# The third batch's mix as seven products, and where its sums and its normalisation stand

## The chip, the cores and the metric

One core of a Trainium2 chip runs the whole kernel in one launch. The metric is device time in microseconds (us). TensorE is written PE, VectorE DVE, ScalarE ACT, GpSimd POOL and SyncE SP, as in the profile.

## The reference

Four batches of 512 rows and 512 columns go through a gated attention block and a gated feed-forward block:

```
q = ctx Wq^T + bq;  k = ctx Wk^T + bk          (256 -> 128)
att = softmax(q k^T)                           (512 x 512)
x = x + tanh(g0) * (LN(x) att^T-mixed over rows: einsum 'bln,bmn->blm')
w = ternary_quant(W): mean(|W|) * clip(round(W / mean(|W|)), -1, 1)
x = x + tanh(g1) * (silu(LN(x) wu^T) * (LN(x) wg^T)) wd^T     (512 -> 2048 -> 512)
```

## The kernel before, in words

Every engine has its program written out by hand, in the order in which it runs, and semaphores with constant counts order the engines against each other. An instruction that waits holds back all that stands behind it on its engine. SP issues all DMAs, transposes included, in one queue.

**Attention, batch by batch.** In batch `b` PE projects the context of batch `b + 1` (`project`, L724), transposes the last tile of the probabilities of `b` (`transpose_p`, L749), computes four tiles of energies of `b + 1` (`energy`, L738), and mixes the rows of `b`. ACT copies the transposed probabilities out of PSUM (`copy_at`, L1111), adds the biases of the next q and k (`bias_qk`, L1095), takes exponentials (`exp_row`, L1102) and scales them (`norm_p`, L1107). Between these ACT sums the absolute values of the weights for the ternary scale (`sum_abs`, L1088), rounds and signs them (L1118, L1124) and makes the high halves of the feed-forward's input (`high_t`, L1143). DVE takes row maxima (`row_max`, L1473), reciprocals of the row sums (`row_rsum`, L1477), mean and variance of the rows coming in (`rows_in`: L1484, L1490) and going out (`stats2`, `aggregate2`, L1515 and L1521; two tiles together in `rows_out`), adds the mix to the rows, normalises (`norm_x1`, L1529) and makes the low halves (`low_t`, L1547). POOL computes the factors of the normalisations in short dependent steps (`rstd1`, `rstd1_two`, `rstd2`, `rstd2_two`).

**The mix** of a batch is a product of 512x512x512 in float32. In the last two batches it is plain: `mix(b, i)` for four row tiles, each of 4 matmuls of 512 columns (L765), and DVE adds a tile of 512 columns (`make_x1`, L1495). In the first two (`b < NS`) it is done in quarters as seven products in place of eight (`mix_product`, L788: 4 matmuls of 256 columns each), in the order `MIX`; each product's result is added with factor `tanh * rstd` to the x tiles by two instructions of 256 columns (`add_mixed`, L1507; `s_xe` counts 14 in a batch). Products 5, 6, 7 and 3 have a sum of quarters of x^T on the left (`x_sums_1`, `x_sums_2`), 5, 6, 7 and 4 one of quarters of the probabilities on the right (`p_sums_1`, `p_sums_2`); POOL makes these eight sums of 512 columns. Products 1 and 2 need no sum.

**Bridge to the feed-forward.** Its input, the normalised x of all four batches, is also cut in quarters with seven products. The quarters and their sums (B11, B21, B22, T1 to T4) are cast to a high half by ACT (`high_t`) and a low half by DVE (`low_t`), and each is transposed by two DMAs (`transpose_block`, L466). POOL makes T3's and T1's differences (L639, L641; semaphores `s_t3`, `s_t1`), DVE those of T2 (L1647) and T4 (L1622). SP also loads W_down in four pieces (`load_down`), x^T tiles (`load_xt`) and writes x tiles of batches 2 and 3 back to DRAM (`spill`, L442). In `T_ORDER` the blocks are B11, B21, T3, T1, T2, B22, T4, and ACT's, DVE's and SP's programs follow it.

**Feed-forward.** From `product1(0)` on PE multiplies with ternary weights (L872, L874) and, from the fourth unit on, the hidden values with W_down. `product3(0)` is the first that waits for ACT's `copy_5(0)` (L1299), which stands behind `copy_1(0)`, T4's high half and a half of a sign on ACT; `copy_1(0)` in its turn waits for T4's difference.

The places on which the change bears, in PE's loop and in ACT's, which the change leaves as it is:

```
if i == 0: act.wait_ge(s_t3, 1); high_t(0, "T3", t3_sb)        # b == 2
if b == 2 and i == 1: act.wait_ge(s_t1, 1); high_t(0, "T1", xf_half(1, 0))
if i == 1: sum_abs(2, 2)                                       # then copy_at, exp_row(3, 3)
if b == NS and i < 2: pe.wait_ge(s_xe, 14 * NS)                # mix(b, i)
```

## Time and profile before

| | us |
|---|---|
| three runs: median (lowest to highest) | 396.78 (396.38 to 397.04) |
| the profiled execution, its own time | 397.08 |
| its span | 395.3 |
| PE busy | 389.9 |
| DVE busy | 314.4 |
| ACT busy | 266.7 |
| POOL busy | 169.3 |
| DMA, mean | 111 GB/s |

The attention of the four batches stands in the first 94 us, the feed-forward behind it. The granted TensorE clock is full in all slices. A busy share is a mean over stretches with different limits; what a step costs is read from the timeline of the engines around it. All times inside the kernel are given from the start of the span.

### The profile page before, as it was taken

Reading aid. Unit: us, or ns where it says so; the run is one execution under the profiler, and the core shown is the slowest. Engines: PE = TensorE matmul, PEld = TensorE weight load, DVE = VectorE, ACT = ScalarE, POOL = GpSimd, SP = SyncE. Lnnn points to the kernel's source line nnn. Section 1 sums busy time; section 2 is a strip of 40 time slices with the busy share of each in tenths; the row PEclk is TensorE's granted clock in tenths of the full one; section 3 lists DMA queues with packets and bytes.
Section 4 is the critical chain, followed back from the end, with each engine's and each line's share of the span. In section 5 each row is a group of like instructions: output and inputs, shape, how many; then the busy total and the mean of one; then the engine's idle time right before and its main releaser. Section 6 shows DMA issues by size and latency. Waiting matters only on the chain.

```text
span 395.3 us, 6059 instructions
## 1 busy us (share of the span) xinstructions
PE 389.9 (99%) x1944; PEld 214.9 (54%) x1952; DVE 314.4 (80%) x475; ACT 266.7 (67%) x360; POOL 169.3 (43%) x187
## 2 busy tenths in 40 slices
PE   8999999999999999999999999999999999999997
PEld 6566775454444444444444444444445565656886
DVE  0768897888899985879897875786869989798974
ACT  3786989889778786869788863746377566654400
POOL 0686826657875013222347002435359446271000
PEclk9999999999999999999999999999999999999999
DMA  7999967598500030030009643041500000000014
GB/s 286 409 413 414 389 210 174 151 266 211 162 2 0 1 108 0 2 107 0 2 0 225 117 79 61 1 167 73 165 22 1 2 2 2 0 2 0 2 55 159
DMA packets 43183, 43.91 MB, mean 111 GB/s; under 512 B 30992, under 2 KB 33168, under 8 KB 41104
## 3 DMA queue, kind: packets, MB, share of 16 engines
q1 hardware_dynamic: 43152, 43.53, 35.4%
q8 instruction: 16, 0.26, 0.3%
q14 instruction: 15, 0.12, 0.1%
HBM read 29.89 MB, written 6.29 MB: 92 GB/s over the span
## 4 chain that ended last, share of the span: by engine, by line
PE 75%; DVE 7%; issue 6%; ACT 5%; POOL 3%; DMA 2%; SPq 1%; DVEq 0%; POOLq 0%; ACTq 0%
PE pair L872 22%; PE pair L874 22%; PE pair L946 14%; PE pair L990 11%; PE pair L788 3%; DMA xf<-in_wdT 2%; PE pair L738 1%; ACT sh L1102 1%; DVE small L1473 1%; PE pair L724 1%; PE pair L803 1%; DMA xf<-in_first 1%; SPq L466 1%; DVE small L1515 1%; DVE xf L1674 1%
## 5 line engine op out<-in xcount | busy, mean ns | idle before, releaser
L872 PE MATMUL pair<-xb_hi,w_sb 128*128 128x512 f16 x448 | 169.8, 379 | 0.4 <-ACT xf L1299 0.2
L874 PE MATMUL pair<-xb_lo,w_sb 128*128 128x512 f16 x448 | 169.8, 379 | 0.0
L872 PEld LDWEIGHTS pair<-xb_hi,w_sb 128*128 128x128 bf16 x448 | 43.8, 98 | 52.9 <-ACT xf L1299 1.1
L874 PEld LDWEIGHTS pair<-xb_lo,w_sb 128*128 128x128 bf16 x448 | 43.8, 98 | 51.1 <-issue 0.3
L1250 ACT ACTIVATE xf<-xf,small 128x512 f32<-128x512 f32 x48 | 34.5, 720 | 52.3 <-DVE xf L1669 31.6
L946 PE MATMUL pair<-x_sb,sh 128*128 128x512 bf16 x248 | 55.1, 379 | 0.4
L1674 DVE SCALAR_TENSOR_TENSOR xf<-xf,small 128x512 f32<-128x512 f32 x48 | 40.0, 836 | 8.4 <-ACT xf L1250 8.4
L946 PEld LDWEIGHTS pair<-x_sb,sh 128*128 128x128 f16 x256 | 24.9, 98 | 30.6 <-DVE x_sb L1711 0.9
L604 POOL TENSOR_TENSOR w_sb<-w_sb 128x512 bf16<-128x512 bf16 x8 | 9.6, 1197 | 63.0 <-ACT w_sb L1124 63.0
L1679 DVE TENSOR_TENSOR sh<-xf,sh 128x512 f16<-128x512 f32 x36 | 32.1, 898 | 0.7 <-ACT sh L1261 0.7
L1725 DVE SCALAR_TENSOR_TENSOR x_sb<-pair,small,x_sb 128x256 f32<-128x256 f32 (+1 forms) x57 | 25.5, 472 | 5.9 <-PE pair L990 5.4
L1711 DVE SCALAR_TENSOR_TENSOR x_sb<-pair,small,x_sb 128x512 f32<-128x512 f32 x32 | 23.9, 747 | 7.8 <-PE pair L946 7.7
L1261 ACT ACTIVATE sh<-xf 128x512 f16<-128x512 f32 x36 | 22.1, 623 | 10.5 <-DVE xf L1674 9.3
L697 POOL TENSOR_TENSOR xf<-xf 128x512 f32<-128x512 f32 x7 | 9.9, 1409 | 44.2 <-DMA xb_lo<-xf 28.1
L765 PE MATMUL pair<-sh,xt_sb 128*128 128x512 f32 (+2 forms) x80 | 28.6, 508 | 0.0
L1664 DVE TENSOR_TENSOR xf<-pair,xf 128x1024 f32<-128x1024 f32 x16 | 19.5, 1221 | 8.8 <-PE pair L874 8.6
L1669 DVE TENSOR_TENSOR xf<-pair,xf 128x1024 f32<-128x1024 f32 x16 | 19.5, 1220 | 4.1 <-PE pair L874 3.9
L1659 DVE TENSOR_TENSOR xf<-pair,xf 128x1024 f32<-128x1024 f32 x16 | 19.5, 1220 | 4.1 <-issue 1.6
L1287 ACT ACTIVATE xf<-pair 128x1024 f32<-128x1024 f32 x16 | 16.4, 1023 | 8.1 <-PE pair L874 7.6
L765 PEld LDWEIGHTS pair<-sh,xt_sb 128*128 128x128 f32 x80 | 13.9, 190 | 12.6 <-issue 10.5
L1674 DVE SCALAR_TENSOR_TENSOR c<-c,small,pair 128x512 f32<-128x512 f32 x16 | 11.9, 742 | 10.1 <-ACT c L1250 10.1
L1118 ACT ACTIVATE w_sb<-w_sb,small 128x1024 f32<-128x1024 f32 x16 | 18.9, 1227 | 0.0
(198 smaller groups left out, 715.9 us busy)
## 6 DMA issues: line engine op xcount, KB each, us to landing
w_sb<-in_wugT SPq DMA_DIRECT2D x8, 1024.0 KB, 14.7
x_sb<-in_x SPq DMA_DIRECT2D x4, 1024.0 KB, 11.3
xf<-in_wdT SPq DMA_DIRECT2D x4, 1024.0 KB, 6.6
xt_sb<-in_wdT SPq DMA_DIRECT2D x4, 1024.0 KB, 5.0
xt_sb<-in_xT SPq DMA_DIRECT2D x12, 256.0 KB, 6.1
x_dram<-x_sb SPq DMA_DIRECT2D x8, 256.0 KB, 3.3
out<-x_sb SPq DMA_DIRECT2D x8, 256.0 KB, 2.0
x_sb<-x_dram SPq DMA_DIRECT2D x2, 1024.0 KB, 5.5
```

The lines of the kernel that those rows point to most:

```text
L765: last = pe.matmul(ps_x[i % 2][:, lo:hi], xt_tile(b, i)[:, k, :], at[:, k, lo:hi], start=(k == 0), stop=(k == KD - 1))
L872: pe.matmul(dst[:, m * 512:(m + 1) * 512], w[:, o:o + P], hi[:, k], start=start and k == 0, stop=False, skip_group_check=not start)
L874: last = pe.matmul(dst[:, m * 512:(m + 1) * 512], w[:, o:o + P], lo[:, k], start=False, stop=k == 1, skip_group_check=not start)
L946: ins = pe.matmul(dst, h_part(n, c, lo)[:, i * P:(i + 1) * P], t_d[:, e * DM + lo_col:e * DM + hi_col], start=first and n == units[0] and ...
L990: ins = pe.matmul(fin_bank(g, j, t), hidden(u, c, lo, min(t, NT - 1)), cols, start=first and u == units[0] and lo == 0 and not (side and t ...
L1250: act.activation(cb(n, c)[:, 0:512], src, ACT.Silu, scale=su[:, :]).then_inc(s_silu[c], 1)
L1261: act.activation(part(n, c, 0), shaped(n, c, cb(n, c)[:, 0:512]), ACT.Copy).then_inc(s_hi[c], 1)
L1659: dve.tensor_tensor(cb(n, "11"), ps_y[:, :], cb(n, "11"), ALU.add).then_inc(s_c["11"], 1)
L1674: dve.scalar_tensor_tensor(cb(n, c)[:, 0:512], cb(n, c)[:, 0:512], kap[:, :], gate, ALU.mult, ALU.mult).then_inc(s_mul[c], 1)
L1679: dve.tensor_tensor(part(n, c, 1), shaped(n, c, cb(n, c)[:, 0:512]), part(n, c, 0), ALU.subtract)\
L1711: dve.scalar_tensor_tensor(y_tile(b, i), at, c_out[:, :], y_tile(b, i), ALU.mult, ALU.add)\
L1725: dve.scalar_tensor_tensor(fin_rows(g, j, t), fin_bank(g, j, t), c_out[:, :], fin_rows(g, j, t), ALU.mult, ALU.add).then_inc(s_ef, 1)
```

## The change

The plain mix of batch 2 becomes seven products (`NS = 3`), so batch 3 alone keeps `mix`. Product 2 changes place with product 5: `MIX` becomes 1, 2, 6, 5, 7, 3, 4 in all three batches. In batch 0 `project(1, 1)` comes before `transpose_p(0, 3)`. The eight sums of batch 2 go into blocks that are free by then: the sums of x^T into `c21`, into a quarter of x^T itself (in place), and into the blocks T3 of `xb_hi` and `xb_lo`; the sums of the probabilities into the place of W_down's first piece. POOL's program is written anew from the sums of batch 0 on; the normalisation factors of batches 2 and 3 are made two tiles at a time. DVE adds batch 2's products, and `norm_x1` of batch 2 moves into batch 3, one tile behind each `make_x1`. SP's queue is put in another order between B21 and T2. ACT's program is unchanged.

The diff, cut to its core:

```diff
-    NS = 2
+    NS = 3
...
-        MIX = (1, 5, 6, 3, 7, 2, 4)
+        MIX = (1, 2, 6, 5, 7, 3, 4)
         MIX_TO = {1: (0, 0), 5: (1, 1), 6: (0, 1), 3: (0, 1), 7: (1, 1), 2: (0, 0), 4: (1, 0)}
         MIX_BEFORE = {2: 1, 3: 6, 7: 5}
         XA = {1: (0, 0), 2: (0, 1), 4: (1, 1), 5: 0, 7: 1, 6: 2, 3: 3}
         def x_sum(b, k):
+            if b == 2:
+                if k == 1:
+                    return x_quarter(b, 1, 0)
+                home = c21[:, :] if k == 0 else (xb_hi, xb_lo)[k - 2][:, 5120:6144].bitcast(F32)
+                return home.rearrange("p (i s) -> p i s", i=2)
             home = xf[:, 6144:8192] if b == 0 else xb_hi[:, 1024:5120].bitcast(F32)
             return home[:, k * 512:(k + 1) * 512].rearrange("p (i s) -> p i s", i=2)
                 if b == 2:
                     sp.wait_ge(s_mp, 7)
                 elif b == 3:
-                    sp.wait_ge(s_xm, i + 1)
+                    sp.wait_ge(s_ss, 4 * b)
+                    sp.wait_ge(s_mp, mixed(2, 2 if i < 2 else 4))
                 sp.dma_start(xt_tile(b, i), xT[b, i]).then_inc(xt_in(b, i)[0], 16)
             def load_ug(m, c):
             for i in range(NT):
                 load_xt(2, i)
             def spill(g):
-                sp.wait_ge(s_x1, g - NS * NT + 1)
+                if g < NS * NT:
+                    sp.wait_ge(s_xe, added(2, 3 if g % NT < 2 else 4))
+                else:
+                    sp.wait_ge(s_x1, g - NS * NT + 1)
                 sp.dma_start(x1_dram[g // NT - 2, g % NT], x_tile(g // NT, g % NT)).then_inc(d_spill, 16)
             def stage_down(c):
                     sp.wait_ge(d_tb[{"T2": "T1", "T4": "T2"}[blk]], 32)
                 if n == 0 and blk == "T3":
                     sp.wait_ge(s_abs, 2 * NABS)
+                    sp.wait_ge(s_mp, mixed(2, 3))
                 if n == NU:
                     sp.wait_ge(s_p[P_OF[blk]], NU)
                 for lo in range(2):
             load_down(2)
             transpose_block(0, "B21")
             load_xt(3, 0)
+            load_xt(3, 1)
+            transpose_block(0, "T3")
             spill(8)
-            load_xt(3, 1)
             spill(9)
-            transpose_block(0, "T3")
+            load_down(3)
             load_xt(3, 2)
-            load_down(3)
+            load_xt(3, 3)
+            transpose_block(0, "T1")
             spill(10)
-            transpose_block(0, "T1")
-            load_xt(3, 3)
             spill(11)
             spill(12)
             transpose_block(0, "T2")
...
             x_sums_1(0)
             hold(pool, s_pn0, NT - 1)
-            x_sums_2(0)
+            x_sum_2(0)
+            p_sum_1(0)
             rstd1_two(0, 0)
-            p_sums_1(0)
+            p_sum_2(0)
             rstd1_two(0, 1)
-            p_sums_2(0)
+            p_sum_3(0)
+            x_sum_4(0)
+            p_sum_4(0)
             x_sums_1(1)
-            x_sums_2(1)
+            x_sum_2(1)
+            x_sum_4(1)
             rstd1_two(1, 0)
             rstd2_two(0, 0)
-            p_sums_1(1)
+            p_sum_1(1)
+            p_sum_2(1)
             rstd1_two(1, 1)
-            p_sums_2(1)
+            p_sum_3(1)
+            p_sum_4(1)
             rstd2_two(0, 1)
-            rstd1(2, 0)
-            rstd1(2, 1)
+            rstd1_two(2, 0)
+            x_sums_1(2)
+            x_sum_2(2)
+            x_sum_4(2)
             rstd2_two(1, 0)
             rstd2_two(1, 1)
+            p_sum_1(2)
+            p_sum_2(2)
+            rstd1_two(2, 1)
+            p_sum_3(2)
             hold(pool, s_x2n, 2 * NT)
             pool.tensor_tensor(t3_sb, xf_half(1, 1), xf_half(1, 0), ALU.subtract).then_inc(s_t3, 1)
+            p_sum_4(2)
             hold(pool, s_t3, 1)
             pool.tensor_tensor(xf_half(1, 0), xf_half(1, 0), xf_half(0, 0), ALU.subtract).then_inc(s_t1, 1)
...
+            rstd1_two(3, 0)
+            pool.wait_ge(s_red, 2)
+            coef(pool.tensor_scalar(kap0[:, :], scale[:, 0:1], XS / HS, 0.0, ALU.mult, ALU.add))
+            coef(pool.tensor_tensor(kap[:, :], kap0[:, :], mone[:, :], ALU.pow))
+            pool.tensor_scalar(su[:, :], scale[:, 0:1], 1.0 / XS, 0.0, ALU.mult, ALU.add).then_inc(s_coef, 1)
+            rstd2_two(2, 0)
+            rstd1_two(3, 1)
+            rstd2_two(2, 1)
             sum_1(0)
...
+                elif j != 2:
+                    pe.wait_ge(s_xe, added(b, {6: 1, 7: 6, 4: 7, 5: 2, 3: 5}[j]))
...
                     project(b + 1, 0)
+                if first:
+                    project(b + 1, 1)
                 transpose_p(b, NT - 1)
-                if not last:
+                if not (first or last):
                     project(b + 1, 1)
                 if b < NS:
                     mix_product(b, 1)
                     energy(b + 1, 0)
                     energy(b + 1, 1)
-                    mix_product(b, 5)
+                    mix_product(b, 2)
                     mix_product(b, 6)
                     transpose_p(b + 1, 0)
                     energy(b + 1, 2)
-                    mix_product(b, 3)
+                    mix_product(b, 5)
                     mix_product(b, 7)
                     if b == 1:
                         pe.wait_ge(s_qk, 5)
                         total(0, 2 * NABS, 2 * NABS, ps_q)
                     transpose_p(b + 1, 1)
                     energy(b + 1, 3)
-                    mix_product(b, 2)
+                    mix_product(b, 3)
                     transpose_p(b + 1, NT - 2)
                     mix_product(b, 4)
                     continue
...
             def stats2(b, i):
                 if b < NS:
-                    hold(dve, s_xe, added(b, 2 if i < 2 else 4))
+                    hold(dve, s_xe, added(b, 3 if i < 2 else 4))
                 else:
                     hold(dve, s_x1, (b - NS) * NT + i + 1)
...
             for b in range(NS):
+                if b == 2:
+                    rows_in(2, 2)
+                    rows_in(2, 3)
                 add_mixed(b, 1)
                 row_max(b + 1, 0)
                 row_max(b + 1, 1)
                 row_rsum(b + 1, 0)
                 row_rsum(b + 1, 1)
-                add_mixed(b, 5)
+                add_mixed(b, 2)
...
-                add_mixed(b, 3)
+                add_mixed(b, 5)
                 row_rsum(b + 1, 2)
                 add_mixed(b, 7)
                 if b == 1:
...
                 row_max(b + 1, 3)
                 if b == 0:
                     rows_in(1, 2)
-                else:
+                elif b == 1:
                     low_t(0, "B11", xf_half(0, 0))
-                add_mixed(b, 2)
+                else:
+                    low_t(0, "T3", t3_sb)
+                add_mixed(b, 3)
                 row_rsum(b + 1, 3)
                 rows_out(b, 0)
                 add_mixed(b, 4)
...
-                else:
+                elif b == 1:
                     norm_x1(1, 0)
                     norm_x1(1, 1)
                     low_t(0, "B21", xf_half(0, 1))
                     norm_x1(1, 2)
                     norm_x1(1, 3)
...
+                else:
+                    rows_in(3, 2)
+                    rows_in(3, 3)
+                    low_t(0, "T1", xf_half(1, 0))
+                    hold(dve, s_t1, 1)
+                    hold(dve, s_tl, t_done(0, "B11"))
+                    dve.tensor_tensor(xf_half(0, 0), t3_sb, xf_half(0, 0), ALU.add).then_inc(s_t2, 1)
+            b = NB - 1
+            for i in range(NT):
+                make_x1(b, i)
+                if i == NT - 1:
+                    hold(dve, s_tl, t_done(0, "B21"))
+                    hold(dve, s_t2, 1)
+                    dve.tensor_tensor(xf_half(0, 1), xf_half(0, 1), xf_half(0, 0), ALU.subtract).then_inc(s_t4, 1)
+                mark2 = stats2(b, i)
+                aggregate2(b, i, mark2)
+                norm_x1(b - 1, i)
+                if i == 0:
+                    low_t(0, "T2", xf_half(0, 0))
+                if i == 1:
+                    low_t(0, "B22", xf_half(1, 1))
             hold(dve, s_t4, 1)
             low_t(0, "T4", xf_half(0, 1))
```

How the order of the instructions changes at the places of which the prediction speaks:

PE, the beginning of batch 2's mix, before (L765 is `mix`, L738 `energy`, L749 `transpose_p`; `xt_sb` holds x^T, `sh` the probabilities, q and k):

```order
L765 MATMUL pair<-sh,xt_sb 128x384 [waits s_xe,d_xt0,s_at]
L765 MATMUL pair<-sh,xt_sb 128x384 x3
L765 MATMUL pair<-sh,xt_sb 128x128 [waits s_at]
L765 MATMUL pair<-sh,xt_sb 128x128 x3
L738 MATMUL pair<-sh 128x512 [waits s_qk]
L738 MATMUL pair<-sh 128x512
L765 MATMUL pair<-sh,xt_sb 128x512 [waits s_xe,d_xt1]
L765 MATMUL pair<-sh,xt_sb 128x512 x3
```

The same place now (L808 is `mix_product`, L758 `energy`, L769 `transpose_p`; `xf` holds sums of the probabilities, `xb_hi` and `c` sums of x^T):

```order
L808 MATMUL pair<-sh,xt_sb 128x256 [waits d_xt1,s_xe,d_xt0,s_at]
L808 MATMUL pair<-sh,xt_sb 128x256 x3
L758 MATMUL pair<-sh 128x512 [waits s_qk]
L758 MATMUL pair<-sh 128x512
L808 MATMUL pair<-sh,xt_sb 128x256 x4
L808 MATMUL pair<-xf,xb_hi 128x256 [waits s_ts,s_ss,s_xe]
L808 MATMUL pair<-xf,xb_hi 128x256 x3
L769 MATMUL pair<-early,sh 128x128 [waits s_at,s_pn]
L769 MATMUL pair<-early,sh 128x128 x3
L758 MATMUL pair<-sh 128x512 [waits s_exp]
```

Four matmuls of 256 columns stand ahead of the wait on `s_qk` where four of 384 and four of 128 stood.

POOL, around T3's difference (`t_sb<-xf`), before; L597 and L598 are `rstd2`, L568 and L569 `rstd2_two`:

```order
L568 TENSOR_SCALAR small<-small 128x2 [waits s_ln2]
L569 TENSOR_TENSOR small<-small 128x2 [waits s_pool]
L639 TENSOR_TENSOR t_sb<-xf 128x1024 [waits s_x2n]
L641 TENSOR_TENSOR xf<-xf 128x1024 [waits s_t3]
L597 TENSOR_SCALAR small<-small 128x1 [waits s_ln2]
L598 TENSOR_TENSOR small<-small 128x1 [waits s_pool]
```

The same place now (L594, L598, L601 and L605 are sums of the probabilities, L560 to L564 `rstd1_two`):

```order
L570 TENSOR_TENSOR small<-small 128x2 [waits s_pool]
L594 TENSOR_TENSOR xf<-sh 128x512 [waits s_at,s_abs]
L598 TENSOR_TENSOR xf<-sh,xf 128x512 [waits s_ts]
L560 TENSOR_SCALAR small<-small 128x2 [waits s_ln1]
L561 TENSOR_TENSOR small<-small 128x2 [waits s_pool]
L562 TENSOR_SCALAR small<-small 128x2 [waits s_pool]
L563 TENSOR_TENSOR small<-small 128x2 [waits s_pool]
L564 TENSOR_SCALAR small<-small 128x2 [waits s_pool]
L601 TENSOR_TENSOR xf<-sh 128x512
L664 TENSOR_TENSOR t_sb<-xf 128x1024 [waits s_x2n]
L605 TENSOR_TENSOR xf<-sh,xf 128x512 [waits s_ts]
L667 TENSOR_TENSOR xf<-xf 128x1024 [waits s_t3]
```

Between the last `rstd2_two` and T3's difference now stand three sums and a `rstd1_two`, and a fourth sum between the two differences.

SP from the transposes of B21 on, before (L466 transposes, L397 loads x^T, L442 writes x tiles back, L411 loads a piece of W_down):

```order
L397 DMA xt_sb<-in_xT 128x512 [waits s_xm]
L442 DMA x_dram<-x_sb 128x512 [waits s_x1]
L397 DMA xt_sb<-in_xT 128x512 [waits s_xm]
L442 DMA x_dram<-x_sb 128x512 [waits s_x1]
L466 DMA_TRANSPOSE xb_hi<-xb_hi 128x8x128 [waits s_abs,s_tl,s_th]
L466 DMA_TRANSPOSE xb_lo<-xb_lo 128x8x128
L397 DMA xt_sb<-in_xT 128x512 [waits s_xm]
L411 DMA xf<-in_wdT 128x2048 [waits s_abs]
L442 DMA x_dram<-x_sb 128x512 [waits s_x1]
```

The same place now (L476 transposes, L403 loads x^T, L451 writes x tiles back, L417 loads a piece of W_down):

```order
L403 DMA xt_sb<-in_xT 128x512 [waits s_mp,s_ss] x2
L476 DMA_TRANSPOSE xb_hi<-xb_hi 128x8x128 [waits s_abs,s_mp,s_tl,s_th]
L476 DMA_TRANSPOSE xb_lo<-xb_lo 128x8x128
L451 DMA x_dram<-x_sb 128x512 [waits s_xe] x2
L417 DMA xf<-in_wdT 128x2048 [waits s_abs]
L403 DMA xt_sb<-in_xT 128x512 [waits s_mp,s_ss] x2
L476 DMA_TRANSPOSE xb_hi<-xb_hi 128x8x128 [waits s_tl,s_th]
L476 DMA_TRANSPOSE xb_lo<-xb_lo 128x8x128
```

The last of W_down's four pieces now stands behind T3's transposes and both writes of batch 2's first x tiles (before, it stood behind T3's transposes and one x^T load). T3's transposes wait for a product too (`s_mp`).

## Rows read from the trace of the kernel before

**Rows 1.** The page's first section: busy time, share and instructions of each engine.

```profile
PE 389.9 (99%) x1944; PEld 214.9 (54%) x1952; DVE 314.4 (80%) x475; ACT 266.7 (67%) x360; POOL 169.3 (43%) x187
```

**Rows 2.** Timeline of PE: start, length, line, operation, tiles, [idle before].

```profile
22.30 3.69 PE L788 MATMUL pair<-xf 128*128 128x256 f32 x16 [0.69 <-POOL xf L585]
...
60.52 3.63 PE L765 MATMUL pair<-sh,xt_sb 128*128 128x384 f32 x16
...
63.99 1.88 PE L738 MATMUL pair<-sh 128*128 128x512 f32 x4
...
79.70 10.51 PE L765 MATMUL pair<-sh,xt_sb 128*128 128x384 f32 x32
...
100.95 0.39 PE L872 MATMUL pair<-xb_hi,w_sb 128*128 128x512 f16 x1 [0.18 <-ACT xf L1299]
```

**Rows 3.** Timeline of ACT in batch 2.

```profile
62.31 1.25 ACT L1095 ACTIVATE sh<-pair,small 128x512 f32<-128x512 f32 x2
...
67.77 1.33 ACT L1107 ACTIVATE sh<-sh,small 128x512 f32<-128x512 f32 x2
...
69.68 1.06 ACT L1143 ACTIVATE xb_hi<-t_sb 128x1024 f16<-128x1024 f32 x1 [0.58 <-DMA xb_lo<-xb_lo]
...
73.97 1.04 ACT L1143 ACTIVATE xb_hi<-xf 128x1024 f16<-128x1024 f32 x1
...
74.92 1.89 ACT L1088 ACTIVATE xf<-xf 128x2048 f32<-128x2048 f32 x1
...
77.29 0.67 ACT L1102 ACTIVATE sh<-pair,small 128x512 f32<-128x512 f32 x1
```

**Rows 4.** Timeline of POOL: two sums, a rstd1_two to the next sum, T3's difference.

```profile
38.86 1.27 POOL L585 TENSOR_TENSOR xf<-sh 128x512 f32<-128x512 f32 x1 [1.30 <-ACT sh L1111]
...
40.27 1.28 POOL L587 TENSOR_TENSOR xf<-sh,xf 128x512 f32<-128x512 f32 x1
...
41.63 0.25 POOL L559 TENSOR_SCALAR small<-small 128x2 f32<-128x2 f32 x1
...
43.82 1.28 POOL L590 TENSOR_TENSOR xf<-sh 128x512 f32<-128x512 f32 x1
...
63.63 2.38 POOL L639 TENSOR_TENSOR t_sb<-xf 128x1024 f32<-128x1024 f32 x1 [1.64 <-DVE xf L1529]
```

**Rows 5.** Timeline of DVE in batches 1 and 2.

```profile
38.74 0.66 DVE L1484 BATCH_NORM_STATS2 small<-x_sb 128x6 f32<-128x512 f32 x1
...
39.61 2.22 DVE L1529 TENSOR_SCALAR xf<-x_sb,small 128x512 f32<-128x512 f32 x2
...
48.32 0.99 DVE L1529 TENSOR_SCALAR xf<-x_sb,small 128x512 f32<-128x512 f32 x2
...
56.47 1.29 DVE L1515 BATCH_NORM_STATS2 small<-x_sb 128x6 f32<-128x512 f32 x2
...
57.96 0.88 DVE L1507 SCALAR_TENSOR_TENSOR x_sb<-pair,small,x_sb 128x256 f32<-128x256 f32 x2
...
62.49 1.00 DVE L1529 TENSOR_SCALAR xf<-x_sb,small 128x512 f32<-128x512 f32 x2
...
65.66 1.27 DVE L1473 TENSOR_REDUCE small<-pair 128x1 f32<-128x512 f32 x2
```

**Rows 6.** Timeline of SP's queue.

```profile
75.19 1.23 SPq L466 DMA_TRANSPOSE xb_hi<-xb_hi  x1
...
77.84 0.58 SPq L397 DMA_DIRECT2D xt_sb<-in_xT  x1
...
78.47 0.44 SPq L411 DMA_DIRECT2D xf<-in_wdT  x1
```

**Rows 7.** The loads of W_down's pieces (L411): from issue to landing, four of them.

```profile
DMA to landing us min/median/max: 5.8/6.6/8.6
```

**Rows 8.** The chain that ended last: start, length, what.

```profile
78.47 6.55 DMA xf<-in_wdT
...
95.40 1.55 DVE xf L1622
```

84 lines of the change are left out of this document (15 added, 69 removed).

## The prediction

> **What bounds the kernel now.** I read the busy shares first, then PE's timeline, then those of ACT, POOL, DVE and SP around batch 2, last the chain that ended last. PE is busy for 389.9 of 395.3 us [rows 1], so what counts is what PE executes and the few places where it waits. Its timeline shows one such place in the attention: 0.69 us idle before 22.30, on a sum by POOL [rows 2]. Batch 2's mix begins at 60.52, the next energies at 63.99, batch 3's mix at 79.70, and the first feed-forward product that waits for ACT (product 3 of unit 0) at 100.95, after 0.18 us of idling [rows 2]. Between 60 and 101 PE has no other gap of note, but its partners run with it tooth on tooth: the chain that ended last leaves PE there and goes by W_down's last piece (DMA from 78.47) and DVE's T4 difference (95.40) to PE again [rows 8]. That is the thing to see: in this stretch two paths are equally long, PE's own and one through ACT, DVE and SP. A saving on PE is kept only if the other path gets shorter too.
>
> **What PE saves.** A plain mix is 16 matmuls of 512 columns, the seven products are 28 of 256. The rate: three tiles take 10.51 us from 79.70, the last one's end modelled, and the first tile of batch 2 takes 3.47 from 60.52 to 63.99 [rows 2]; I take 3.45 a tile and half of it, 1.72, a product. 4 x 3.45 less 7 x 1.72 is **1.7 us** less work. That is 0.43% of the time, against about 0.2% (0.8 us) that a measurement of this kernel can tell from no change.
>
> **Product 2 second (batches 0 to 2).** It needs no sum, so batch 0's 0.69 us idle before 22.30 goes [rows 2]. What is late next: POOL now makes a sum of the probabilities ahead of the normalisation factors for which DVE's first addition waits, 1.23 us at the pace of two sums running (38.86 and 40.27 are 1.41 apart with a dependence, 1.27 long each) [rows 4], and that sum needs the fourth transposed tile, which now stands behind a projection of 1.72 us. DVE's row maxima behind that addition come about 1 us later, and with them the exponentials and PE's next transpose. I take 0 for the whole; the ends are -1.2 (all gained) and +0.5. In batch 1 PE has no gap and I see none: 0.
>
> **Batch 2, wait by wait**, from PE's 60.52:
>
> 1. Product 1 is done at 60.52 + 1.72 = 62.24. The energies of batch 3 need the biased q and k. ACT does both biases from 62.31 for 1.25 us [rows 3], and its program is unchanged and was busy before. So PE waits till 63.6: **+1.37**. Before, 3.47 us of mix hid that with 0.4 to spare; now 1.7 of it is gone. This alone takes back most of the saving.
> 2. DVE used to wait for PE here; now it runs from its two normalisations at 62.49 [rows 5] into `rows_in` for two tiles, 0.87 each (38.74 to 39.61) [rows 5]. But POOL's first two new sums of the probabilities begin at 62.55, just behind ACT's copy. Two `norm_x1` beside such sums took 2.22 us, from 39.61, and 0.99 without, from 48.32 [rows 4, 5]. I take +0.9, nearer the first row, since this is the same pair of operations; the other end is 0. The Trainium skill (SBUF — State Buffer, "SBUF: two separate sides") says that DVE and POOL share a port pair, and whichever begins first keeps it for its whole instruction; were DVE always first, the wait would fall on POOL and the sum would be 0.5 us less. So `rows_in` ends at 66.05, the first addition begins there, row maxima at 66.85. Before they began at 65.66 and the scaled row for PE's transpose was ready at 67.77 + 0.7 [rows 3, 5]: now 69.7. PE, done with products 2 and 6 at 68.8, waits **0.9**.
> 3. POOL: the factors for tiles 2 and 3 need `rows_in`, so 66.2 to 68.4 (2.19 from 41.63 to 43.82), a sum of 1.23, then T3's difference of 2.38 [rows 4]: ready at 72.0 in place of 66.0. T1's difference comes behind one more sum: 72.0 + 1.2 + 2.4 = 75.6. ACT's unchanged program has T3's high half (69.68 before, held there by a DMA) and T1's (73.97) ahead of `sum_abs` (74.92) and of the exponential of the last energies (77.29) [rows 3]. Now: T3 at 72.15, T1 at 75.75, `sum_abs` at 76.7, exponential at 76.7 + 2.37 = 79.05, done 0.87 later, at 79.9.
> 4. DVE takes that row's reciprocal ahead of `rows_out` and of the last addition (product 4). `rows_out` takes 1.49 (56.47 to 57.96), the addition 0.88 [rows 5]: 80.1 + 1.49 + 0.88 = 82.5. Batch 3's mix waits for all 42 additions. So it begins at **82.5, not 79.70: +2.8**. Before it waited for no such addition. In PE's terms: -1.7 work, then waits of 1.37, 0.9, 1.4 (the transpose behind ACT's last scaling) and 1.1 (the addition), less 0.2 of waits that were there.
>
> **Batch 3 and the bridge.** From 79.70 to 100.95 are 21.25 us with 0.18 idle [rows 2]. With nothing else late, product 3 of unit 0 comes at 82.5 + 21.07 = 103.6: +2.6. The other path: T3's low half stands behind the last row maximum. PE's last energies of batch 3 end at 75.8, maximum and low half take 0.7 and 1.2, and T3's transposes are issued at 77.8 (75.19 before). They take SP 2.65, two writes 0.5 each, so W_down's last piece is asked for at 81.5, 3.0 later than 78.47 [rows 6]. It landed in 6.55 [rows 8]; the quickest of the four took 5.8 [rows 7]; it has less company now, so the path from there on, 22.5 us to product 3, gives +2.2 to +3.0. In DVE's chain from there two `norm_x1` at 0.5 replace one `rows_in` at 0.87: 0. The middle of the second is the first's +2.6; I take that for both. Moving the loads and writes on SP costs nothing besides: x^T's last two tiles, asked for at 82, are needed at 89 and later.
>
> **The feed-forward** keeps its order, so what is late at product 3 stays late. Making the factors two at a time saves POOL time where it isn't waited for: 0.
>
> **Sum.** On the profiled execution (397.08, span 395.3) +2.6 gives 399.7. The median of the three runs stands 0.3 lower, 396.78, so I predict **399.4**. Without the collision of step 2 it is +1.7, 398.5; with all of batch 0's gain too, 397.3; with waits at their upper ends +3.5, 400.3.
>
> **Rivals.**
>
> *The gain arrives.* Time follows PE's work: -1.7, with batch 0's gap -2.4, so 394.4 to 395.1. It would need the biases and the last exponential to be out of PE's way. For it: PE's 99%. Against: 62.31 + 1.25 in ACT's rows, and an unchanged ACT program. It decides if PE's energies start by 62.3. Chance 0.13, with partial gains. [...]
>
> *It cancels.* T3's difference does come late but ACT had slack, so the last exponential stays at 77.29 + 0.87. Then `rows_out` and the addition still end at 80.7: +1.0 at batch 3's mix, less 0.18 and batch 0's 0.69: +0.1, 396.9. Against: ACT's row at 69.68 leaves T3 2.3 us less than it needs. Chance 0.14.
>
> *It gets worse at SP.* T2's transposes wait until T1's have landed, and T1's are now asked for at 86, when DVE has made the low half behind `rows_out` and `rows_in`; B22's are behind T2's and product 3 needs them. I find 101 to 102 for their landing, 1.5 us ahead of need; a landing as slow as W_down's slowest (8.6 for a median of 6.6 [rows 7]) makes it a wait of 1 to 2 more: 400.8. Chance 0.17.
>
> *The forecast*, three waits in a row behind ACT and DVE: 0.56.
>
> **How the numbers follow.** The likeliest is 399.4. The range, 396.0 to 401.2, takes in cancelling and most of the worse case and leaves out the gain (0.13) and a tail above (0.06). Faster is the gain, 0.13; same the cancelling case, 0.14; slower the other two, 0.73.
>
> **What would show it.** PE: a gap of 1.4 before batch 3's first energies, about 1 before its first transpose, and batch 3's mix at 82 to 83, released by DVE's addition. ACT: waits on POOL ahead of T3's and T1's high halves. DVE: idle 2 us before the last reciprocal of batch 3's rows. Batch 0: no gap at 22, but one before the first transpose at 25. Wrong it would be if PE showed no gap between 60 and 83, or if batch 3's mix began before 80.

## The result

Four timed runs of each on one chip: **404.67 us** after (404.64 to 405.97), 396.91 us before (396.38 to 397.16); ratio **1.0195**, interval 1.0181 to 1.0210. The change makes the kernel 2% slower: the forecast had the direction, but 404.67 lies 3.5 us above its range (396.0 to 401.2). The profiled run took 404.69, with a span of 402.9 (395.3 before).

The page of the changed kernel, busy shares, against [rows 1]: PE's busy time is the same, its share is not, so the 7.6 us are time in which PE stands idle.

```profile
PE 389.9 (97%) x1960; PEld 218.4 (54%) x1968; DVE 321.4 (80%) x485; ACT 266.6 (66%) x360; POOL 173.5 (43%) x179
```

PE's timeline of the changed kernel, for [rows 2] (start, length, line, operation, tiles, idle before):

```profile
60.03 1.89 PE L808 MATMUL pair<-sh,xt_sb 128*128 128x256 f32 x8
63.11 1.98 PE L758 MATMUL pair<-sh 128*128 128x512 f32 x4 [1.19 <-ACT sh L1117]
64.93 1.89 PE L808 MATMUL pair<-sh,xt_sb 128*128 128x256 f32 x8
69.50 3.39 PE L808 MATMUL pair<-xf,xb_hi 128*128 128x256 f32 x8 [2.69 <-DVE x_sb L1529]
72.73 0.60 PE L769 MATMUL pair<-early,sh 128*128 128x128 f32 x4
...
83.38 0.65 PE L769 MATMUL pair<-early,sh 128*128 128x128 f32 x4 [0.54 <-ACT sh L1129]
84.94 10.58 PE L785 MATMUL pair<-sh,xt_sb 128*128 128x384 f32 x32 [0.91 <-DVE x_sb L1529]
96.29 3.67 PE L785 MATMUL pair<-sh,xt_sb 128*128 128x512 f32 x8 [0.65 <-DVE x_sb L1517]
105.98 0.39 PE L894 MATMUL pair<-xb_hi,w_sb 128*128 128x512 f16 x1 [0.59 <-ACT xf L1299]
108.87 0.39 PE L894 MATMUL pair<-xb_hi,w_sb 128*128 128x512 f16 x1 [0.99 <-ACT xf L1321]
```

Three stretches, each the difference of two starts. **Batch 2**, from product 1 to batch 3's mix: 24.91 us (60.03 to 84.94), before 19.18: +5.7. **The bridge**, from that mix to product 3 of unit 0 (the row at 108.87): 23.93, before 21.25: +2.7. Before batch 2 -0.5, behind product 3 -0.3. Sum +7.6. The -0.5 is no gain: in the versions below whose program up to there is the same, product 1 starts between 60.03 and 60.84.

In batch 2 PE waits four times: for ACT's biases (1.19), ahead of product 6 (2.69), for the last transpose (0.54), for the last addition (0.91). And product 6 itself takes 3.23 us to the next row where products take 1.72. The windows of the changed kernel say why (per stretch: busy time of PE, PEld, DVE, ACT, POOL, then PEclk, the granted clock):

```profile
62.00:70.00 8.00, 4.21 (x13) 2.69 (x14) 7.79 (x13) 3.32 (x4) 5.21 (x6) 0.93 1.00 263
70.00:74.00 4.00, 4.00 (x14) 2.91 (x14) 3.01 (x10) 2.67 (x6) 3.67 (x5) 0.70 0.00 0
74.00:80.00 6.00, 6.00 (x29) 4.90 (x28) 4.74 (x12) 4.81 (x7) 5.45 (x7) 1.00 0.00 0
```

In windows of 1 us the granted clock is 0.98 from 68 to 69 and 0.50 from 69 to 72: in the 2.69 us wait it fell from its upper level (2.4 GHz) to the lower (1.2 GHz). So product 6 took PE 1.5 us more. Whether the kernel paid for that is another question, taken up with *fill* below.

What was late ahead of product 6 is on POOL and DVE. POOL's timeline of the changed kernel, for [rows 4]:

```profile
55.34 1.27 POOL L575 TENSOR_TENSOR c<-xt_sb 128x512 f32<-128x512 f32 x1 [2.63 <-DMA xt_sb<-in_xT]
...
59.43 1.27 POOL L588 TENSOR_TENSOR xb_lo<-xt_sb,xb_hi 128x512 f32<-128x512 f32 x1
60.79 0.19 POOL L569 TENSOR_SCALAR small<-small 128x2 f32<-128x2 f32 x1
...
63.00 2.21 POOL L594 TENSOR_TENSOR xf<-sh 128x512 f32<-128x512 f32 x1
65.35 1.27 POOL L598 TENSOR_TENSOR xf<-sh,xf 128x512 f32<-128x512 f32 x1
...
72.17 2.37 POOL L664 TENSOR_TENSOR t_sb<-xf 128x1024 f32<-128x1024 f32 x1
...
75.72 2.37 POOL L667 TENSOR_TENSOR xf<-xf 128x1024 f32<-128x1024 f32 x1
```

DVE's timeline of the changed kernel, for [rows 5]:

```profile
61.94 1.00 DVE L1551 TENSOR_SCALAR xf<-x_sb,small 128x512 f32<-128x512 f32 x2 [1.93 <-POOL small L570]
62.85 1.22 DVE L1569 TENSOR_TENSOR xb_lo<-xf,xb_hi 128x1024 f16<-128x1024 f32 x1
63.99 2.92 DVE L1551 TENSOR_SCALAR xf<-x_sb,small 128x512 f32<-128x512 f32 x2
...
68.58 0.88 DVE L1529 SCALAR_TENSOR_TENSOR x_sb<-pair,small,x_sb 128x256 f32<-128x256 f32 x2
```

And the chain that ended last, for [rows 8], enters this stretch by a load and leaves it by another, that of W_down's last piece:

```profile
42.63 12.54 DMA xt_sb<-in_xT
...
63.99 2.92 DVE xf L1551 x2
...
84.66 6.25 DMA xf<-in_wdT
```

So batch 2's x^T, asked for behind two of W_down's pieces and x, lands at 55.3. POOL's four x^T sums stand behind it and ahead of the factors (L569) of batch 1's last norms, so DVE idles 1.93 us. Then the instructions of DVE and POOL mesh: POOL's sum (63.00) waits out DVE's low half, and DVE's next two norms (63.99) wait out that sum and the one behind it: 2.21 for 1.27, and 2.92 for 1.00. The first addition starts at 68.58.

**The bridge's 2.7 us** split in three by DVE's rows. T2's low half in the kernel before, and in the changed kernel with ACT's sum over W_down's last piece ahead of it and B22's low half behind it:

```profile
88.09 1.23 DVE L1547 TENSOR_TENSOR xb_lo<-xf,xb_hi 128x1024 f16<-128x1024 f32 x1 [0.84 <-ACT xb_hi L1143]
```

```profile
90.93 1.91 ACT L1110 ACTIVATE xf<-xf 128x2048 f32<-128x2048 f32 x1 [2.85 <-DMA xf<-in_wdT]
...
93.98 1.50 DVE L1569 TENSOR_TENSOR xb_lo<-xf,xb_hi 128x1024 f16<-128x1024 f32 x1 [1.26 <-ACT xb_hi L1165]
...
98.00 2.17 DVE L1569 TENSOR_TENSOR sh<-xf,sh 128x1024 f16<-128x1024 f32 x1
```

T2's low half starts 9.04 us behind the mix, before 8.39: +0.65, since W_down's last piece was asked for 6.2 us later than before, where the mix started only 5.2 us later, and ACT waited 2.85 us for it (before 1.14). The two low halves take 1.2 us more, beside POOL's weight sums. And DVE has two norms (97.17 and 101.86) ahead of T4's difference where it had one `rows_in`, 0.86 us more. From the end of T4's difference to product 3 are 4.0 us in both kernels.

### The profile page after: what moved, and what is told of

Its sections match the earlier page's. It is cut to its first block, busy times and chain, and to the rows that moved or that the text cites. A ratio compares the mean times of both kernels' runs of the same rounds, so it can differ in the third digit from the quotient of the medians.

```text
span 402.9 us, 6102 instructions
## 1 busy us (share of the span) xinstructions
PE 389.9 (97%) x1960; PEld 218.4 (54%) x1968; DVE 321.4 (80%) x485; ACT 266.6 (66%) x360; POOL 173.5 (43%) x179
## 4 chain that ended last, share of the span: by engine, by line
PE 73%; DVE 7%; issue 5%; DMA 5%; POOL 4%; ACT 4%; SPq 1%; DVEq 0%; POOLq 0%; ACTq 0%
PE pair L894 21%; PE pair L896 21%; PE pair L968 14%; PE pair L1012 11%; DMA xt_sb<-in_xT 3%; PE pair L808 2%; DMA xf<-in_wdT 2%; PE pair L758 1%; DVE xf L1551 1%; PE pair L744 1%; DVE small L1506 1%; PE pair L819 1%; ACT sh L1124 1%; DVE small L1495 1%; DVE xf L1682 1%
## 5 line engine op out<-in xcount | busy, mean ns | idle before, releaser
L1682 DVE SCALAR_TENSOR_TENSOR xf<-xf,small 128x512 f32<-128x512 f32 x48 | 41.4, 866 | 7.0 <-ACT xf L1272 6.9
L1687 DVE TENSOR_TENSOR sh<-xf,sh 128x512 f16<-128x512 f32 x36 | 30.8, 862 | 0.7 <-ACT sh L1283 0.7
L1719 DVE SCALAR_TENSOR_TENSOR x_sb<-pair,small,x_sb 128x512 f32<-128x512 f32 x32 | 23.9, 748 | 8.2 <-PE pair L968 8.2
L1283 ACT ACTIVATE sh<-xf 128x512 f16<-128x512 f32 x36 | 22.2, 624 | 9.0 <-DVE xf L1682 7.7
L1309 ACT ACTIVATE xf<-pair 128x1024 f32<-128x1024 f32 x16 | 16.3, 1022 | 9.7 <-PE pair L896 9.7
L1529 DVE SCALAR_TENSOR_TENSOR x_sb<-pair,small,x_sb 128x256 f32<-128x256 f32 x42 | 18.4, 479 | 4.2 <-POOL small L564 2.8
L1299 ACT ACTIVATE xf<-pair 128x1024 f32<-128x1024 f32 x16 | 16.2, 1011 | 5.8 <-DVE xf L1653 2.5
## 6 DMA issues: line engine op xcount, KB each, us to landing
x_sb<-in_x SPq DMA_DIRECT2D x4, 1024.0 KB, 12.2
```

Source lines behind the costliest of these rows:

```text
L1283: act.activation(part(n, c, 0), shaped(n, c, cb(n, c)[:, 0:512]), ACT.Copy).then_inc(s_hi[c], 1)
L1682: dve.scalar_tensor_tensor(cb(n, c)[:, 0:512], cb(n, c)[:, 0:512], kap[:, :], gate, ALU.mult, ALU.mult).then_inc(s_mul[c], 1)
L1687: dve.tensor_tensor(part(n, c, 1), shaped(n, c, cb(n, c)[:, 0:512]), part(n, c, 0), ALU.subtract)\
L1719: dve.scalar_tensor_tensor(y_tile(b, i), at, c_out[:, :], y_tile(b, i), ALU.mult, ALU.add)\
```

## Experiments

Each has 4 to 10 runs, compared with the kernel before on the same chip. The medians of the kernel before are 396.5 to 397.6 there, so versions from different batches are compared by their ratios. The span is that of its profiled run; "batch 2" is the stretch from product 1 to batch 3's mix.

**1. Product 2 second in batches 0 and 1 alone** (the kernel before with `MIX`, the projection and POOL's sums in the new order there).

> The kernel before with one part of the change: product 2 second in batches 0 and 1, POOL's order of batches 0 and 1, and the projection ahead of the last transpose. The changed kernel reached its first matmul of batch 2 at 60.03 us against 60.52 before. If batch 2's part alone made the kernel slower, this one is 0 to 0.5 us faster than before (396.4 to 396.9). The rival, that product 2 second or POOL's new order already costs something further on, gives over 397.7.

Measured 396.98, ratio 1.0003 (0.9989 to 1.0016). The gap at 22 is only moved, as PE's timeline shows; the term of 0 was right.

```profile
23.80 1.97 PE L800 MATMUL pair<-xf 128*128 128x256 f32 x8 [0.17 <-POOL xf L591]
26.22 0.66 PE L761 MATMUL pair<-early,sh 128*128 128x128 f32 x4 [0.45 <-ACT sh L1121]
```

**2. The four steps ahead of product 6**, each undone alone in the changed kernel: SP loads batch 2's x^T ahead of W_down's pieces and x (*x^T first*); POOL holds its p sums until DVE's norms are done (*no collision*); PE runs six needless matmuls of 256 columns in its wait (*fill*); ACT's `sum_abs(2, 1)` goes behind the biases (*biases first*).

```diff
+            for i in range(NT):
+                load_xt(2, i)
             load_down(0)
...
+            pool.wait_ge(s_x2n, 2 * NT)
             p_sum_1(2)
...
+                        for _ in range(6):
+                            pe.matmul(ps_pt[0][:, 0:256], ones[:, :], k_sb[:, 0:256], start=True, stop=True)
...
                     if b == 2:
+                        sum_abs(2, 1)
                         round_unit(0)
```

> The changed kernel with batch 2's x^T asked for ahead of W_down's first two pieces and of x of batch 3. Theory: POOL's sums of x^T waited 2.6 us for that load (until 55.3), which held back the factors for batch 1's normalisation, DVE's normalisations, its first addition and PE. Then the sums begin at 52.7, DVE's first norm_x1 of batch 1 at 60.0 in place of 61.9, and the time falls by 1.5 to 2.5 us, to 402.2 to 403.2. Rival: the load is hidden, since DVE and POOL collide later anyway; then 404.2 to 404.9.

> The changed kernel with POOL's first sum of batch 2's probabilities held until DVE has done the eighth norm_x1. Theory: DVE's last two normalisations took 2.92 us beside two sums by POOL where they take 1.0 alone; apart, DVE gains 1.9, the first addition comes at 66.7 in place of 68.6, and PE's product 6 is then held by the second sum of the probabilities (about 67.8) instead: PE gains 1.0 to 1.7, and the time is 403.0 to 403.8. Rival: the order of the two does not matter, because POOL's delay is worth as much as DVE's: 404.4 to 405.5.

> The changed kernel with six needless matmuls of 256 columns put into PE's wait of 2.7 us ahead of product 6 of batch 2. Theory: product 6 took 3.2 us from its start to the next one's in place of 1.72, since the granted clock fell behind the wait (mean 0.91 from 62 to 80 us); with PE kept busy it takes 1.72 and PE is 1.5 us earlier at its end, but the next transpose waits for ACT's scaled row (ready at 72.2), so the time falls by 0 to 0.5, to 404.2 to 404.7. Rival: product 6 is slow for its operands (sums in other blocks), and stays at 3.2.

> The changed kernel with ACT's second sum of W_down's absolute values moved behind the biases of batch 3. The bias wait on PE (1.2 us before 63.11) goes. Theory: it was hidden, since product 6 waits for DVE's first addition at 68.6 in any case, so the time stays within 0.5 us, 404.2 to 405.2. Rival, the prediction's sum, in which this wait is a term of 1.4: 403.2 to 403.6.

*x^T first:* 403.65 (1.0159, 1.0127 to 1.0191), -1.0, which is not clear of the noise: the four runs lie at 402.91 twice, 404.39 and 404.99. The last of these is the profiled one. In it POOL's wait for the load is gone (sums from 53.53), but the third sum then met DVE's low half (2.25), W_down's piece and with it ACT's biases came later, and the collision at 64 stayed: norms of 3.03.

*No collision:* 402.63 (1.0139, 1.0117 to 1.0162), **-2.0**. The norms take 1.00, product 6 waits 0.74, and the clock of this run stays at its upper level throughout (the other three have a mean of 0.996, as the changed kernel has):

```profile
64.39 1.00 DVE L1552 TENSOR_SCALAR xf<-x_sb,small 128x512 f32<-128x512 f32 x2
```

```profile
68.38 1.97 PE L809 MATMUL pair<-xf,xb_hi 128*128 128x256 f32 x8 [0.74 <-POOL xf L598]
```

Batch 2 takes 23.58 us, 1.3 less than in the changed kernel, since the last transpose now waits 1.97 us. The larger part of the gain stands in the bridge, 22.12 us for 23.93, whose program is the same: W_down's last piece is asked for at 83.00 and lands 5.3 us later, ACT waits 0.74 us for it in place of 2.85, and DVE does not wait ahead of T2's low half.

*Fill* (it adds six matmuls whose result nobody reads): 403.43 (1.0164, 1.0138 to 1.0191), -1.2, with more work on PE. Product 6 starts no earlier, at 69.84, but takes 1.99, and the clock of the same windows is 1.00:

```profile
62.00:70.00 8.00, 6.50 (x26) 4.64 (x26) 7.52 (x12) 3.43 (x5) 5.28 (x7) 1.00 0.99 250
70.00:74.00 4.00, 3.25 (x15) 2.21 (x16) 3.01 (x9) 2.67 (x6) 3.52 (x6) 1.00 0.07 27
```

It shows that the slow product came from the idle before it, and not from its operands. Its batch 2 is not shorter (25.12): the next transpose waited for ACT's scaled row and started at 72.58, in the changed kernel at 72.73. From DVE's first addition (68.91, in the changed kernel 68.58) to batch 3's mix are 16.36 us in both traces. So up to the mix the slow product cost nothing: PE's waits behind it were shorter by as much. What this run won stands in the bridge (22.20 us), where the waits of 0.65 and 0.59 are missing; its piece of W_down, asked for at 84.56, landed 5.4 us later in place of 6.3. That the clock brought this is not shown. Runs of one version say a little more: in *swap*, *three* and *late* some have a mean clock of 1.000 and some of 0.996, and the latter are longer by 0.6, 0.45 and 0.95 us, from four runs each.

*Biases first:* 404.71 (1.0204, 1.0185 to 1.0223), nothing. PE's 1.19 us wait for the biases lay in front of a longer one (3.74 us ahead of product 6 once it was gone), so the term of 1.37 was no term.

**3. POOL's order; the last row's order; biases, POOL and swap together (*three*).** POOL makes the factors before the second x^T sum, holds the p sums, and makes T3's difference ahead of `rstd1_two(2, 1)`, the third p and fourth x^T sums (*POOL*). DVE takes `rows_out(2, 0)` ahead of the last reciprocal (*swap*).

```diff
             x_sums_1(2)
+            rstd2_two(1, 0)
             x_sum_2(2)
-            x_sum_4(2)
-            rstd2_two(1, 0)
             rstd2_two(1, 1)
+            hold(pool, s_x2n, 2 * NT)
             p_sum_1(2)
             p_sum_2(2)
+            pool.tensor_tensor(t3_sb, xf_half(1, 1), xf_half(1, 0), ALU.subtract).then_inc(s_t3, 1)
             rstd1_two(2, 1)
```

> The changed kernel with POOL's program of batch 2 in another order: the factors of batch 1's normalisation ahead of the later sums of x^T, the sums of the probabilities held until DVE's normalisations are done, T3's difference right behind the second of them. Theory: POOL's order and its meeting with DVE are the main cause; the first addition comes at 65 to 66 in place of 68.6, product 6 starts at 66.5 to 67 at full clock, T3's high half is made at 69 in place of 74.6, batch 3's mix starts at 81 to 82 in place of 84.9, and the time is 399.5 to 401.5. Rival: ACT's or the bridge's chain takes over and gives most of it back: over 402.5.

> The changed kernel with DVE's outgoing statistics of batch 2's first two tiles ahead of the reciprocal for the last row of batch 3. Theory: product 4's addition waited for the exponential; it comes 0.7 us earlier, batch 3's mix too (84.2), and the time falls by 0.3 to 1.0, to 403.7 to 404.4. Rival: W_down's last piece, asked for at 84.7, ends last in any case, so nothing changes: 404.4 to 404.9.

> All three: biases first, POOL's new order, DVE's statistics first. Theory: with batch 2's waits gone the 1.7 us of PE work appear at least in part; batch 3's mix starts at 78.5 to 80, and the time is 396 to 398. Rival: the bridge (W_down's last piece, the high and low halves, DVE meeting POOL's weight sums) holds product 3 as much as in the changed kernel behind its start, 23.9 us, 2.7 more than before: 398.5 to 400.5.

*POOL:* 402.42 (1.0139, 1.0124 to 1.0155), **-2.25**; product 6 runs without a wait. *Swap:* 404.39 (1.0193, 1.0178 to 1.0208), -0.3, within the noise. *Three:* 401.97 (1.0133, 1.0116 to 1.0150), batch 2 in 22.27; it came out above both its theory and its rival. Taking the waits ahead of product 6 away brought up the next, ACT's for T1's difference, with PE's last transpose behind it. ACT's and PE's timelines with POOL's order:

```profile
77.21 1.06 ACT L1165 ACTIVATE xb_hi<-xf 128x1024 f16<-128x1024 f32 x1 [2.90 <-POOL xf L667]
```

```profile
82.47 0.66 PE L769 MATMUL pair<-early,sh 128*128 128x128 f32 x4 [2.76 <-ACT sh L1129]
84.03 2.59 PE L785 MATMUL pair<-sh,xt_sb 128*128 128x384 f32 x4 [0.91 <-DVE x_sb L1529]
```

**4. T1's difference on DVE; batch 2's norms late; T4's difference early.**

On the changed kernel, batch 2's four norms leave batch 3's loop and stand ahead of the ternary steps of units 0 to 3 (*late*). On top of *three*, T1's difference moves from POOL to DVE, and `rows_out(2, 0)` goes behind the last addition (*T1 on DVE*); then the norms too (*both*); then T4's difference goes from the last tile to behind B22's low half.

```diff
                 row_rsum(b + 1, 2)
+                if b == 2:
+                    hold(dve, s_t3, 1)
+                    dve.tensor_tensor(xf_half(1, 0), xf_half(1, 0), xf_half(0, 0), ALU.subtract).then_inc(s_t1, 1)
                 add_mixed(b, 7)
...
-                norm_x1(b - 1, i)
...
+                    norm_x1(2, n)
                     ternary_down(n)
```

> The changed kernel with one thing moved: batch 2's four normalisations leave VectorE's fourth batch and stand ahead of the four steps that make the ternary W_down pieces in units 0 to 3. Theory (they are what lengthened the bridge from the start of batch 3's mix to product 3 of unit 0 from 21.25 to 23.93 us): three of them stand ahead of T4's difference (0.50 + 0.90 + 0.90 in the trace of the change), and two low halves that met GpSimd's weight sums (1.50 and 2.17 where 1.22 is theirs alone) are met otherwise; the bridge is near 21.5 and the kernel near 402.5 (-2.2). Rival (GpSimd's weight sums collide with whatever VectorE does there, and the load of W_down's last piece, 6.2 us after an issue 3.5 us later than before, sets the second half's T2): bridge stays above 23, time 404 to 404.7.

> The version with the bias, GpSimd-order and reciprocal edits together (401.97), with T1's difference computed by VectorE (1.22 us, in its 0.86 us wait ahead of product 7's addition) in place of GpSimd (2.35 us, ready at 77.2), and the first two row sums of batch 2 behind the last addition. Theory (T1's difference holds ScalarE 2.76 us and so the last transpose and batch 3's mix): T1's high half at 74.5, the last exponential at 77.5, transpose(3,3) at 79.7 in place of 82.05, batch 3's mix at 80.2 in place of 82.54, time 399.7 (-2.3). Rival (the last piece of W_down and VectorE's own list, not the mix's start, set the bridge): the mix starts near 80 but product 3 of unit 0 stays at 105 to 106, time 401.2 to 402.

> The two together: bias, GpSimd-order, T1 on VectorE, and batch 2's normalisations ahead of the ternary steps. Theory (the start of batch 3's mix and the bridge behind it are two separate losses): mix at 80.2, product 3 of unit 0 at 101.7 to 102.2, time 397.3 to 398. Rival (they share one cause, VectorE's list, so that the second brings little on top of the first): 399 to 399.7.

> As the version with both, and T4's difference taken behind B22's low half, ahead of the sums of batch 3's last two tiles. Theory (in the bridge the last wait of TensorE is that for the copy behind T4's difference): T4's difference ends by 95, the copy of product 1 starts with product 1's end, no wait above 0.3 us ahead of product 3; time 0.5 to 1 us under the version with both, 396.5 to 397.2, so level with the kernel before. Rival (the two sums delayed by 1.2 us hold the last tile's mix through its bank): TensorE waits 0.5 to 1 us ahead of batch 3's last tile in place of it, and the time is the same within 0.3.

*Late alone:* 404.70 (1.0201, 1.0185 to 1.0216): nothing in the time. The bridge itself did get shorter, 22.46 us for 23.93, by the rows of PE:

```profile
85.44 10.58 PE L785 MATMUL pair<-sh,xt_sb 128*128 128x384 f32 x32 [0.91 <-DVE x_sb L1529]
...
107.90 0.39 PE L894 MATMUL pair<-xb_hi,w_sb 128*128 128x512 f16 x1 [0.53 <-ACT xf L1321]
```

So the norms were part of the cause. It was less than the 2.4 I expected, since T2's low half waited longer for ACT (1.75 in place of 1.26) and a collision with POOL's weight sums moved to T4's difference. And 1.3 us came back behind product 3 (295.3 us to the end, 294.0 in the changed kernel), where the norms now stand ahead of the ternary steps and PE waits 0.65 us for DVE at 150.45. DVE's timeline of that run, T4's difference (1.52 in the changed kernel):

```profile
101.72 2.18 DVE L1653 TENSOR_TENSOR xf<-xf 128x1024 f32<-128x1024 f32 x1
```

*T1 on DVE:* 401.91 (1.0130, 1.0111 to 1.0149). Batch 2 took 20.66, 1.6 less than with the three, and none of it reached the end: the mix itself now stopped for a load that the later start had covered, and again for DVE:

```profile
88.88 3.70 PE L783 MATMUL pair<-sh,xt_sb 128*128 128x512 f32 x8 [0.98 <-DMA xt_sb<-in_xT]
93.40 3.67 PE L783 MATMUL pair<-sh,xt_sb 128*128 128x512 f32 x8 [0.70 <-DVE x_sb L1515]
```

*Both:* 401.24 (1.0113, 1.0092 to 1.0134). *With T4's difference early:* 401.25 (1.0115, 1.0095 to 1.0136), no change; its profiled run had no wait of PE in the bridge and took 399.89, the least of its six, the others up to 402.24.

**5. ACT's `sum_abs(2, 2)` ahead of T1's high half (*abs*); the DMA queue (*queue*, below); both, and no norm in unit 3 (*best*).**

```diff
             load_xt(3, 1)
+            load_down(3)
             transpose_block(0, "T3")
+            load_xt(3, 2)
+            load_xt(3, 3)
             spill(8)
             spill(9)
-            load_down(3)
-            load_xt(3, 2)
-            load_xt(3, 3)
```

> The version with T4's difference early, with ScalarE's sum over W_down's third piece ahead of T1's high half (it needs no T1). Theory (ScalarE waits 1.42 us for T1's difference with that sum of 1.90 us queued behind it, and the last exponential behind both): the last exponential at 78.0 in place of 78.9, transpose(3,3) at 79.9 to 80.1 in place of 80.81, batch 3's mix at 80.4 to 80.6 in place of 81.30, time 0.7 to 0.9 under that version (401.25), 400.4. Rival (VectorE's last addition of the seven products is next in line at once): the mix starts within 0.3 us of 81.30 and the time stays.

> The version with T4's difference early, with the DMA queue's order changed: W_down's last piece asked for ahead of T3's transposes (by 76 to 79 in place of 81.9), x^T of batch 3's last tiles ahead of the spills. Theory (the piece's landing no longer holds ScalarE, which waits 1.70 us for it in the bridge): T2's high half 1 to 1.7 us earlier, VectorE's 0.80 wait ahead of T2's low half gone; but TensorE has no wait there in that version, so the time changes by no more than 0.3 us. Rival (those waits do reach TensorE): 0.8 us less.

> Both of those, and batch 2's four normalisations spread over units 0 to 2, none in unit 3, where TensorE waited 0.65 us for VectorE's evictions. Theory: mix at 80.5, no wait behind it, the 0.65 in unit 3 gone: span 398.1 - 0.8 - 0.65 = 396.6, time near 399.7 by the median of the parent version, 398.4 by its profiled run. Against the kernel before (mix at 79.70, span 395.3) that is still slower, since the seven products of batch 2 with their waits take as long as the plain mix did. Rival (the waits removed come back further on): 401.

*Abs:* 402.74 (1.0141, 1.0118 to 1.0164), **+1.5** by the medians and 1.0 by the ratios, whose intervals overlap, though its mix starts 1.1 us earlier. PE's timeline:

```profile
80.17 7.14 PE L783 MATMUL pair<-sh,xt_sb 128*128 128x384 f32 x24
89.73 5.40 PE L783 MATMUL pair<-sh,xt_sb 128*128 128x512 f32 x8 [2.42 <-DMA xt_sb<-in_xT]
```

Again a wait of over 2.4 us and slow matmuls behind it (5.40 us for what takes 3.67). *Queue:* 399.34 (1.0069, 1.0051 to 1.0088), **-1.9**, against my theory's 0.3. The edit moves two things: batch 3's x^T, for which the profiled run of the version before did not wait, and W_down's last piece, for which ACT waited 1.70 us there and now does not wait. Either may have stood in the slower runs of that version; which of them did is not shown. *Best:* **399.11** (1.0061, 1.0040 to 1.0082), batch 2 in 20.00, span 397.2.

**6. The waits left in that version.** *Last* moves three norms ahead of unit 0, T1's low half behind batch 3's first sum, ACT's last exponential ahead of two copies and of T1's high half, and POOL's fourth x^T sum ahead of its p sums. *Final* takes that sum back and puts T1's high half behind the last copy. *Spill* takes T1's low half back, puts `rows_in(3, 2)` and `(3, 3)` behind batch 3's first sum, and lets no spill stand between T1's, T2's and B22's transposes.

```diff
             weight_scale(2, 3, ps_pt[0], 3)
+            for i in range(NT - 1):
+                norm_x1(2, i)
```

> The version with all moves so far (399.11; span 397.2), with its remaining waits of TensorE taken one by one: (a) the last exponential ahead of two copies and of T1's high half, and the fourth x^T sum of GpSimd in its 1.70 us wait, so that it no longer meets T1's difference on VectorE (2.13 us where 1.22 is its own): transpose(3,3) without wait (0.43 gone), mix at 79.9 in place of 80.29; (b) T1's low half behind batch 3's first sum: the 0.49 us in the bridge gone; (c) batch 2's normalisations into VectorE's 1.63 us wait ahead of unit 0: the 0.65 us in unit 3 gone. Theory (the waits found in the trace are all of what is left): 1.2 to 1.5 us less, span 395.8, median 396.6 to 398, level with the kernel before. Rival (each wait removed is followed by another in the same place, as with the first versions): 398.7 to 399.5.

> The last version (400.16, span 397.3) with two of its moves corrected by its own trace: GpSimd's fourth x^T sum back behind T3's difference (moved ahead it met VectorE's norms, 1.75 and 1.95 us, and product 6 waited 1.92 us), and T1's high half behind the last copy, which TensorE had waited for 0.62 us ahead of batch 3's mix. Theory (GpSimd's 512-column sums beside VectorE's norms are what costs in batch 2, wherever they stand): product 6 at 66.3 with 0.67 wait, transpose(3,3) by 79.6 and mix by 80.1, no wait of 0.49 and 0.65 behind: span 395.9, median 397.3 to 398.2, that is 0.2 to 0.5% above the kernel before, or level with it. Rival (another wait comes up in the place of each, as in every version so far): 398.7 to 399.5.

> The last version (median 399.35, six runs at 399.16 to 400.11 with spans of 397.3 to 398.3, and the profiled one at 397.38 with a span of 395.6) with the DMA queue freed in the bridge: T1's low half taken again ahead of batch 3's first sum and the row sums of x for tiles 2 and 3 behind it, so that T1's transposes are issued near 85 in place of 88.38; the four spills that stood between T1's, T2's and B22's transposes moved out from between them, so that B22's go at 93 to 94 in place of 96.64. Theory (the 2 us by which most runs lie above the profiled one are TensorE's wait for B22's transposes, 0.41 us in the profiled run at 101.26, and larger where they land later): the wait is gone, all runs lie within 1 us, median 397.3 to 398, span 395.2. Rival (the spread has another source, which the profiled run does not show): median 399 to 399.7 again.

*Last:* 400.16 (1.0064, 1.0043 to 1.0085), by its ratio level with *best*. The mix to the end took 315.7 us, as before the change (315.6); but POOL's fourth sum, moved into its wait, met DVE's norms (1.95) and product 6 waited 1.92. *Final:* 399.35 (1.0052, 1.0038 to 1.0065); its profiled run took 397.38 with a span of 395.6, the six others 399.16 to 400.11. *Spill:* 399.62 (1.0080, 1.0063 to 1.0097), all runs 398.96 to 400.45: the spread was not B22's transposes. In its trace the three norms ahead of unit 0 take 3.23 us where they take 1.55 in *final*, ACT's work behind them is late, and PE waits 1.17 at 115.37, which the profiled run of *final* did not have. That this is the 2 us is not shown.

PE in batch 2 of *final*, which at 20.05 us is within 0.05 of the quickest here (*best*, 20.00):

```profile
59.67 1.89 PE L806 MATMUL pair<-sh,xt_sb 128*128 128x256 f32 x8
...
65.69 1.97 PE L806 MATMUL pair<-xf,xb_hi 128*128 128x256 f32 x8 [0.68 <-POOL xf L598]
67.99 0.66 PE L767 MATMUL pair<-early,sh 128*128 128x128 f32 x4 [0.34 <-ACT sh L1127]
...
71.50 1.96 PE L806 MATMUL pair<-xf,xt_sb 128*128 128x256 f32 x8 [0.26 <-POOL xf L601]
...
79.09 0.66 PE L767 MATMUL pair<-early,sh 128*128 128x128 f32 x4 [0.43 <-ACT sh L1127]
79.72 10.58 PE L783 MATMUL pair<-sh,xt_sb 128*128 128x384 f32 x32
```

and in *spill* at the end of the stretch, where the transpose does not wait:

```profile
77.63 1.89 PE L806 MATMUL pair<-xf,xt_sb 128*128 128x256 f32 x8
79.36 0.60 PE L767 MATMUL pair<-early,sh 128*128 128x128 f32 x4
80.58 10.58 PE L783 MATMUL pair<-sh,xt_sb 128*128 128x384 f32 x32 [0.63 <-ACT sh L1131]
```

*Final* needs 20.05 us from product 1 to the mix, the plain mix 19.18. By the rows' starts, three waits (0.68, 0.34, 0.26 idle) cost 0.86, 0.58 and 0.43: 1.9 us, more than the 1.7 saved. The other 0.8 is the last addition, which stands bare: from product 4 (76.76 in *final*) to the mix are 2.96 and 2.95 us, whether the transpose waits or not, where product and transpose take 1.72 and 0.44. In both runs the mix starts 0.14 to 0.15 us behind the end of DVE's last addition (79.57 and 80.44), as in the changed kernel, though the row of *spill* names ACT. Without the three waits the stretch would take 18.2, an estimate; no version reached it, and none beats the kernel before.

## Why the prediction was wrong

The measured time lies 5.3 us above the forecast. Step 2 accounts for 2.4 of them, the bridge for 2.7.

- *PE's work, -1.7:* the rate is right by the rows, 1.72 us from one product to the next. The busy time shows it badly: 389.9 us as before, where product 6 ran 1.5 us long, 389.4 in *no collision*, where the clock did not fall, and 388.4 in *final*.
- *Batch 0, 0:* right (experiment 1).
- *Step 1, the biases, +1.37:* the wait is there (1.19), but it cost nothing (biases first). I added waits in a row whose later one contained the earlier: the first addition set product 6, whenever the energies ran.
- *Step 2, +0.9:* **the step that failed.** The collision I had sized at 0.9 extra on the pair of norms was 1.9, and there were two things I had not looked for: where x^T's load lands (12.5 us after its issue, so POOL's sums begin at 55.3) and that `rstd2_two` stands behind those sums, so that the norms start at 61.94 only because of POOL and meet its first p sum. "The first addition at 66.05" was 68.58: 1.5 us because the second pair of norms started at 63.99 and not at 62.49, and 1.0 because the meeting was longer. PE's wait came ahead of product 6, 2.69 us, not at the transpose. Undoing the collision gave 2.0 us, POOL's order 2.25. In batch 2 alone it was 1.3 and 1.6, the rest came in the bridge. That the load alone matters is not shown: asked for earlier, it gave 1.0 us, within the noise.
- *No step at all:* the granted clock behind that wait, 1.5 us of slow matmuls. Up to batch 3's mix it was hidden behind ACT and DVE (16.36 us from the first addition to the mix with it and without it, *fill*), so it is not the step that failed. Whether it costs anything behind the mix is open.
- *The rule of the Trainium skill* cited at step 2 (SBUF — State Buffer, "SBUF: two separate sides"), that whichever of DVE and POOL begins first keeps the shared port pair for its whole instruction: the trace agrees. POOL's 63.00 sum ended at 65.21, about one sum behind DVE's low half (64.07). DVE's two norms took about 1.5 us each and ended some 0.3 behind POOL's two sums (65.21 and 66.62). I used the rule for the lower end of the term; it allows a chain of such waits as well, and the chain was longer than my estimate.
- *Step 3:* T3's difference ended at 74.54 (72.0 said) and T1's at 78.09 (75.6), both late by what step 2 was short. Their order was right, and with step 2's wait gone T1's became the next wait as described (2.90).
- *Step 4, +2.8 at the mix:* mechanism right, the addition stood bare (0.91); size +5.2 (84.94 against 79.70). The 2.4 us above the 82.5 of the forecast are those of step 2.
- *The bridge, +2.6 taken over unchanged:* **the second step that failed**; it grew by 2.7. DVE's low halves (1.50, 2.17) met POOL's weight sums, 1.2 us. "Two `norm_x1` replace one `rows_in`: 0" was 0.86, for they took 0.90 each there and not 0.5. And the other path that I had described, by W_down's last piece, was the one that ended last: the piece was asked for at 84.66 (81.5 said), as T3's transposes were issued at 80.88 (77.8 said), and T2's low half came 0.65 us later behind the mix. The bridge's length also depends on when its parts meet: with the same program there it took 22.1 us in *no collision*, 22.2 in *fill* and 23.9 in *biases first*. Of the moves made for it, the norms late gave 1.5 us in the bridge and lost 1.3 behind it, T4's difference early gave nothing in the median, and the queue's order gave 1.9.
- *Rivals:* "worse at SP" had the sign and not the place. Not B22's transposes but W_down's last piece stood in the changed kernel's chain, and batch 3's x^T showed as a wait once the mix came earlier (0.98 in *T1 on DVE*, 2.42 in *abs*).

What stays open: 0.5 to 0.6% between the best versions and the kernel before, about which the one profiled run of each says nothing; why runs of one version differ by up to 2.7 us (those of the kernel before differ by 1.3 to 2.5 us on one chip, so this need not come from the change); and why W_down's last piece lands 5.3 us after its issue in one version and 6.7 in another (*T1 on DVE*).

## What to carry to other kernels

When work is moved onto a second engine, find the load that its first instruction waits for and list what stands behind that instruction on its queue, before sizing anything. Waits in a row do not add: the path that ends last at each product counts, and a wait is a term only if the one behind it moves too. A gain is to be looked for by stretches: here what was moved in batch 2 was in part paid out in the bridge, by loads and meetings that fell otherwise. And where DVE and POOL both stream wide tiles, price each meeting at up to a full instruction of the other, in both directions.

## What was not expected of the hardware

- A wait of PE of 2.69 us was followed by matmuls at half the granted clock, which took 1.5 us more, one of 2.42 us by matmuls that took 1.7 us more. Waits of up to 2.26 us (*x^T first*, *swap*) were not, in any profiled run looked at here. Behind two of 2.75 and 2.76 us the clock stayed in *three* and fell in *POOL*. With needless matmuls in the wait the clock stayed up, and the kernel was 1.2 us faster in spite of them, though the traces do not show that it was the clock that brought it.
- DVE and POOL stretch each other's instructions by up to whole lengths, and such waits form chains: 1.27 to 2.21, then a pair of norms from 1.00 to 2.92, in one place.
- The loads of x^T, 256 KB each, land in 6.2 us in the median of twelve; those of batch 2, asked for behind 3 MB of others, took 12.2 to 12.5. The trace of the kernel before had 10.9 for the same loads, so this could have been read ahead of the forecast.
